# Query constants, transposition and last normalisation reordered, and the gated global row added to the residual by an accumulating transfer

## The reference

```
h   = layernorm(x) * (1 + ca) + sa
# attention inside segments of 128 tokens:
local      = softmax(Q K^T * scale) V              # per segment
global_out = attention over the 16 segments' first rows of the sequence
x   = x + ga * ((local + global_out[segment]) Wo + bo)
h   = layernorm(x) * (1 + cb) + sb
# 16 experts, each token goes to its best one, at most 512 tokens per expert
x   = x + gb * gate * (relu(h W1[e] + b1[e]) W2[e] + b2[e])
```

## Time and profile before

| | us |
|---|---|
| median of three runs | 1887.14 |
| the three runs | 1886.38 to 1889.94 |
| profiled execution | 1889.13 |
| span of its instructions | 1887.4 |

### The profile page before, as it was taken

One profiled execution on the slowest core, in us unless ns is written; L12 is line 12 of the kernel. 1 busy time (PEld: TensorE's weight loads), 2 busy tenths in 40 slices (PEclk: granted clock), 3 DMA queues, 4 the chain that ended last, 5 costly groups with the idle time before them and its releaser, 6 DMA issues.

```text
span 1887.4 us, 28151 instructions
## 1 busy us (share of the span) xinstructions
PE 1796.1 (95%) x9137; PEld 1486.9 (79%) x9138; DVE 1225.6 (65%) x1882; ACT 822.7 (44%) x1322; POOL 870.3 (46%) x709
## 2 busy tenths in 40 slices
PE   8999999999999549999999999999998999999998
PEld 3677787787787437888888888888888988888886
DVE  4568888888887753556554554537658886455762
ACT  2544554544554322433433343335545564334541
POOL 2145655656665441334343432416636757233632
PEclk9999999999999879999999999999999999999999
DMA  8322432342242524343535434345545455434622
GB/s 276 140 92 90 138 131 90 119 149 89 103 166 89 178 68 160 130 142 125 190 134 180 146 123 144 116 157 190 175 142 205 164 210 182 155 123 156 215 88 67
DMA packets 137915, 270.77 MB, mean 143 GB/s; under 512 B 17633, under 2 KB 18221, under 8 KB 137862
## 3 DMA queue, kind: packets, MB, share of 16 engines
q1 hardware_dynamic: 115338, 221.27, 33.6%
q0 software_dynamic: 22528, 48.86, 8.1%
HBM read 237.71 MB, written 50.72 MB: 153 GB/s over the span
## 4 chain that ended last, share of the span: by engine, by line
PE 77%; DVE 14%; issue 4%; ACT 3%; DMA 1%; POOL 0%; DVEq 0%; POOLq 0%; ACTq 0%; SPq 0%
PE bank L328 23%; PE bank L330 23%; PE bank L329 23%; PE bank L773 3%; DVE prob L1271 2%; DVE h L1377 2%; DVE xr L1381 2%; DVE stats L1156 2%; PE bank L715 1%; DVE u_lo L1399 1%; PE bank L816 1%; PE bank L598 1%; PE bank L536 1%; PE bank L587 1%; DVE h_lo L1438 0%
## 5 line engine op out<-in xcount | busy, mean ns | idle before, releaser
L1438 DVE TENSOR_TENSOR h_lo<-h_f,h_hi 128x512 fp32r<-128x512 f32 x256 | 221.3, 885 | 363.4 <-ACT h_f L1090 363.2
L1089 ACT ACTIVATE h_hi<-bank,b_col 128x512 fp32r<-128x512 f32 x256 | 176.4, 689 | 599.6 <-PE bank L330 582.1
L328 PE MATMUL bank<-bt_hi,w_hi 128*128 128x512 f32 (+4 forms) x1024 | 360.3, 352 | 8.4 <-DVE w_lo L1409 5.6
L330 PE MATMUL bank<-bt_hi,w_lo 128*128 128x512 f32 (+4 forms) x1024 | 359.4, 351 | 0.0
L329 PE MATMUL bank<-bt_lo,w_hi 128*128 128x512 f32 (+4 forms) x1024 | 359.4, 351 | 0.0
L328 PE MATMUL bank<-w_hi,h_hi 128*128 128x512 f32 x832 | 326.9, 393 | 3.3 <-DVE h_lo L1438 2.5
L329 PE MATMUL bank<-w_lo,h_hi 128*128 128x512 f32 x832 | 325.4, 391 | 0.0
L330 PE MATMUL bank<-w_hi,h_lo 128*128 128x512 f32 x832 | 324.9, 391 | 0.0
L328 PEld LDWEIGHTS bank<-bt_hi,w_hi 128*128 128x128 f32 x1024 | 194.7, 190 | 33.6 <-issue 9.6
L329 PEld LDWEIGHTS bank<-bt_lo,w_hi 128*128 128x128 f32 x1024 | 194.7, 190 | 21.0
L330 PEld LDWEIGHTS bank<-bt_hi,w_lo 128*128 128x128 f32 x1024 | 194.7, 190 | 20.3
(11 more groups left out here) (265 smaller groups left out, 3220.4 us busy)
## 6 DMA issues: line engine op xcount, KB each, us to landing
raw<-in_L_ffn_W_dram SPq DMA_DIRECT2D x128, 1024.0 KB, 5.5
xa<-in_L_attn_x_dram SPq DMA_DIRECT2D x16, 1024.0 KB, 5.3
xr<-in_L_attn_x_dram SPq DMA_DIRECT2D x16, 1024.0 KB, 8.1
out_dram<-xr SPq DMA_DIRECT2D x16, 1024.0 KB, 10.2
h_rows<-h SPq DMA_DIRECT2D x16, 1024.0 KB, 4.3
b_bc<-in_L_ffn_b_dram SPq DMA_DIRECT2D x16, 256.0 KB, 6.2
wm_a<-in_L_wmod_dram SPq DMA_DIRECT2D x2, 1024.0 KB, 11.1
wm_b<-in_L_wmod_dram SPq DMA_DIRECT2D x2, 1024.0 KB, 11.2
```

Source lines behind the costliest of these rows:

```text
L328: pe.matmul(o, a_hi, b_hi, start=start, stop=False)
L330: return pe.matmul(o, a_lo, b_hi, start=False, stop=stop)
L1089: act.activation(h1_hi[b % 2][:, j, :], h_bank[j][:, :], ACT.Relu, bias=bias)
L1438: dve.tensor_tensor(h1_lo[b % 2][:, j, :], h1_f[:, j, :], h1_hi[b % 2][:, j, :].bitcast(F32), ALU.subtract) \
```

## The change

Five things are edited.

1. The global row leaves PE. The prologue multiplies each global row by its `ga` row (a new product GAROW on PE, a copy on ACT, one multiplication on DVE in place of the four that split the row in three) and stores 64 float32 rows. In each iteration POOL issues a transfer that adds the four rows of group n-1 to the residual `xr`, each row to all 128 partitions; DVE waits for it (`xr_summed`) where it waited for the load of `xr`. The matmul L745, its two tiles and SP's load of `grows` go.
2. `query_const` is taken apart: three of its four rows stand right after `stats1`, the fourth after the second statistics, and the scaling after `u_lo` 0.
3. PE transposes the next `xa` before it multiplies the expert logits.
4. ACT does `modulate` before the fourth `normalise2`.
5. The scratch output of the query rows gets a tile of its own.

```diff
             if cur:
-                wait_past(sp, av_full, 4 * i.n - 4)
-                sp.dma_start(grows[i.par][0:3 * GS, :], global_dram[bass.ds(i.n * 3 * GS, 3 * GS), :]) \
-                    .then_inc(grows_in[i.par], 16)
...
-                    split3(pe, big[s][:, :], pt_hi[:, s, :], pt_lo[:, s, :], u_hi[:, s, :], u_lo[:, s, :], True, False)
-                    pe.matmul(big[s][:, :], seg_sel[:, s, :], grows[p1.par][:], start=False, stop=True) \
+                    split3(pe, big[s][:, :], pt_hi[:, s, :], pt_lo[:, s, :], u_hi[:, s, :], u_lo[:, s, :], True, True) \
                         .then_inc(av_full, 1)
...
+            if cur and not g_tiles:
+                pe.wait_ge(pro_evac, PRO_END)
+            if nxt:
+                transpose_xn(i.plus(1), False)
             if prev2:
                 pe.wait_ge(h2t_done, 4 * p2.n + 4)
...
-            if nxt:
-                transpose_xn(i.plus(1), False)
...
                 empty_u(3)
+            if nxt:
+                modulate(i.plus(1))
             if prev:
                 normalise2(3)
-            if nxt:
-                modulate(i.plus(1))
...
                 stats1(i.plus(1))
+            if cur:
+                for s in range(GS - 1):
+                    query_row(i, s)
...
-                dve.wait_ge(xr_in[p1.par], 16 * (p1.half + 1))
+                dve.wait_ge(xr_summed[p1.par], 16 * (p1.half + 1))
...
             if cur:
+                query_row(i, GS - 1)
                 for s in range(GS):
-                    if s == 2:
-                        query_const(i)
                     dve.wait_ge(u_hi_done, 4 * n + s + 1)
                     dve.tensor_tensor(u_lo[:, s, :], big[s][:, :], u_hi[:, s, :].bitcast(F32), ALU.subtract) \
                         .then_inc(u_split, 1)
+                    if s == 0:
+                        query_const(i)
...
+            def add_global():
+                pool.wait_ge(xr_in[p1.par], 16 * (p1.half + 1))
+                stand_alone(pool, pool_passed)
+                part = global_dram[bass.ds(p1.n * GS, GS), :].unsqueeze(0).to_broadcast([P, GS, D])
+                pool.dma_start(xr[p1.par][:], part, accum_op=ALU.add).then_inc(xr_summed[p1.par], 16)
+            first = isinstance(i.n, int) and i.n == 1
+            if prev and not first:
+                add_global()
             if nxt:
                 normalise1(i.plus(1))
+            if first:
+                pool.wait_ge(g_stored, 16)
+                add_global()
```

More of the change, by code:

```diff
@@ L123, in build_block @@
     ones = keep("ones", [P, P], BF16)
-    seg_sel = keep("seg_sel", [P, GS, P], BF16)
-    grows = [keep(f"grows{i}", [P, D], BF16) for i in range(2)]
+    seg_batch = keep("seg_batch", [NBATCH, NSEG], F32)
     QUAD = P // KC
@@ L179, in build_block @@
     prob, pt_hi, pt_lo = over(r_p, ("prob", seg_sq, F32), ("pt_hi", seg_sq, F32R), ("pt_lo", seg_sq, F32R))
-    logit_parts, = over(cursor[0], ("logit_parts", [P, ROWS], F32))
+    logit_parts, qc_junk = over(cursor[0], ("logit_parts", [P, ROWS], F32), ("qc_junk", [P, D], F32))
     batch_rows = [P, NBATCH, D]
@@ L199, in build_block @@
                                       ("bqk", [NBATCH, 2, D], F32), ("hg_t", [P, KC, NSEG], F32))
-    g_split, brow, u_row, gg_t = over(r_tab + 8 * KB, ("g_split", [NSEG, 3, D], BF16), ("brow", [P, D], F32),
+    g_ga, brow, u_row, gg_t = over(r_tab + 8 * KB, ("g_ga", [NSEG, D], F32), ("brow", [P, D], F32),
                                       ("u_row", [1, D], F32), ("gg_t", [P, KC, NSEG], F32))
@@ L263, in build_block @@
     gsum_masked, gsum_negb, gsum_exp, gsum_prob = (sem(f"gsum_{k}") for k in ("masked", "negb", "exp", "prob"))
-    g_split_done, g_stored, table_cleared = sem("g_split_done"), sem("g_stored"), sem("table_cleared")
+    g_gated, g_stored, table_cleared = (sem(k) for k in ("g_gated", "g_stored", "table_cleared"))
     x_in = [sem(f"x_in{i}") for i in range(2)]
     xr_in = [sem(f"xr_in{i}") for i in range(2)]
-    grows_in = [sem(f"grows_in{i}") for i in range(2)]
+    xr_summed = [sem(f"xr_summed{i}") for i in range(2)]
     ln1_step, ln1_ready, ln1_rstd, xn_done = (sem(k) for k in ("ln1_step", "ln1_ready", "ln1_rstd", "xn_done"))
@@ L346, in build_block @@
     POOL_MADE = 9
-    DVE_MADE = 9
+    DVE_MADE = 7
     def results_done(eng, e, b):
@@ L658, in _ @@
         product(PGT, pe.transpose(pro_bank(PGT)[:, 0:NSEG], pg[:], ident[0:NSEG, 0:NSEG]))
+        pe.wait_ge(mod_fixed, 2)
+        pe.wait_ge(made, POOL_MADE)
+        bank_free(GAROW)
+        product(GAROW, pe.matmul(pro_bank(GAROW)[0:NSEG, :], seg_batch[:], modr[:, GA, :], start=True, stop=True))
         pe.wait_ge(brow_ready, 1)
@@ L1263, in _, with query_row @@
         dve.wait_ge(made, POOL_MADE)
-        def query_const(g):
-            b = batch_of(g)
-            for s in range(GS):
-                if s > 0:
-                    dve.wait_ge(qc_raw, 4 * g.n + s)
-                dve.scalar_tensor_tensor(out=qc_junk, in0=xa[g.par][:, s, :], scalar=1.0,
-                                         in1=vc_tab[:, bass.ds(b, 1), :].rearrange("p b d -> p (b d)"), op0=ALU.mult,
-                                         op1=ALU.mult, accum_out=QRAW[:, s:s + 1]).then_inc(qc_raw, 1)
+        def query_row(g, s):
+            wait_past(dve, qc_raw, 4 * g.n + s)
+            dve.scalar_tensor_tensor(out=qc_junk[:], in0=xa[g.par][:, s, :], scalar=1.0,
+                                     in1=vc_tab[:, bass.ds(batch_of(g), 1), :].rearrange("p b d -> p (b d)"),
+                                     op0=ALU.mult, op1=ALU.mult, accum_out=QRAW[:, s:s + 1]).then_inc(qc_raw, 1)
+        def query_const(g):
             dve.wait_ge(qc_raw, 4 * g.n + 4)
-            dve.tensor_scalar(QCS2[g.par], QRAW, qc_bc[:, bass.ds(b, 1)], SCALE, ALU.add, ALU.mult) \
+            dve.tensor_scalar(QCS2[g.par], QRAW, qc_bc[:, bass.ds(batch_of(g), 1)], SCALE, ALU.add, ALU.mult) \
                 .then_inc(qc_ready, 1)
-        dve.wait_ge(g_split_done, 1)
         tok4 = [P, GS, E]
```

36 lines of the change are left out of this document (13 added, 23 removed).

## The result

The changed kernel takes 1896.38 us (median; 1893.87 to 1897.36), the kernel before 1889.65 beside it: 1.0033 of its time, 95% interval 1.0022 to 1.0044. That is slower by a third of a per cent, where 1880.4 was forecast; the sign was wrong.

A forecast was written before the change was run, and what follows sets the result against it. PE was taken to bound the attention part. -12.6 - 2.8 - 0.5 + 0 + 5.0 + 3.7 + 0.5 = -6.7 us, from the median 1887.14 to 1880.4 us; range 1869 to 1908.

The forecast's parts named there:

- Reordered end of an iteration, -12.6: Attention loop: transposing before the expert logits ends PE's wait for `u_lo`, 0.9 us gained in each of 14 iterations.
- The rival in which another input holds PE just as long: Loop: fourth `u_lo` or POOL's `h2` rows hold PE, only the transfer's costs stay; +6, 1893 us, chance 0.05.
- the prediction's own signs of being wrong: Loop: DVE's first `h` released by the transfer every iteration, or `pt_lo` no longer waiting for ACT; no size given.
- Matmul removed, -2.8: Loop, PE: 0.93 us of matmul saved per iteration, of which 0.2 was credited in each of iterations 2 to 15.
- The same transfer in iteration 1, +5.0: Iteration 1: the transfer, issued behind POOL's normalisation, delays `u` from 108.86 to 113.9; 5.0 us lost once.
- T: Accumulating transfer's time from issue to landing, taken as 6.0 us alone, between 4.7 and 7.3.
- The end, +3.7: Iteration 16: the transfer takes 10 us where DVE wants the sum after 6.3; 3.7 us lost.
- Steady transfer, 0: Steady iterations: the accumulating transfer is hidden before the next first `h`; 0 us.
- The 8.6: Steady iterations: the transfer's forecast time from issue to landing beside the store of `h2`, 8.6 us.
- The rival of a late transfer: Every iteration: the transfer lands after DVE wants it; about 1901 to 1916 us, chance 0.20.
- Query rows beside POOL's normalisation: Loop, DVE's gap: query rows collide with POOL's normalisation; as a rival all three collide, +7, 1894 us, chance 0.13.
- the prologue: Prologue and iteration 0: earlier transposition of group 1 less the added product and copy; 0.5 us gained.

The follow-up runs named there:

- the run with both transfers early: The changed kernel with the accumulating transfers of iteration 1 and of the last group (15) issued earlier; 1881.81 us, 0.9960 of the kernel before.
- the 1252.5 with the query rows put back: The kernel with first and last transfer early, its query rows put back between the second and third `u_lo`; 1910.63 us, 1.0117 of the kernel before.

## Why the prediction was wrong, step by step

- **Reordered end of an iteration, -12.6.** This step failed. The transposition's wait went as worked out, and `ht_lo` started 1.46 us earlier (14.60 after `h` against 16.06). But it ended only 0.49 earlier: its four instructions met more of POOL's scaling, which kept its place, and went from 1.27 to 1.74 us each. The end stayed because it hangs on POOL: 0.55 us behind the sixth scaling operation, which itself ended only 0.49 earlier (20.77 after `h` against 21.26). The prediction had POOL off the path with 1.65 us to spare; through `ht_lo` its scaling was on it. So 0.9 us an iteration became 0.2. The prediction asked what was due next on PE and named the fourth `u_lo`; what was due next was DVE's `ht_lo`, which the trace of before already shows stretched (213 to 570 us; the first row, beside its neighbour of equal size):

```profile
L1217 DVE TENSOR_TENSOR ht_lo<-ht,ht_hi 128x512 fp32r<-128x512 f32 x40 | 50.1, 1267 | 8.1 <-ACT ht L957 7.7
L1399 DVE TENSOR_TENSOR u_lo<-bank,u_hi 128x512 fp32r<-128x512 f32 x40 | 25.5, 678 | 0.0
```

  The rival in which another input holds PE just as long, given 0.05, had the right shape; it named the `h2` rows as PE's input, where POOL's scaling of them acts through `ht_lo`. One of the prediction's own signs of being wrong came true: `pt_lo` waits for ACT 0.5 us in 13 iterations, where it was 29.6.
- **Matmul removed, -2.8.** 0.06 to 0.12 us an iteration with the old orders (36.02 to 35.96 and 35.90), nothing on top of the new ones (35.79 to 35.81), where the period hangs on the end of `ht_lo` and DVE's chain from there to `h`.
- **The same transfer in iteration 1, +5.0.** Right in place, too small: moving it away saved 11.2. T was 8.3 and not 6.0, `h` can come 1.9 us earlier than in the kernel before (104.65 against 106.57), and the sum had no term for PE's clock after the stall, 1.9 on PE and at most 0.7 in the time.
- **The end, +3.7.** 3.3 by the run with both transfers early.
- **Steady transfer, 0.** Right. It lands 10.2 us after its issue at 423.61, near 433.8, and `h` starts at 435.73. The 8.6 was too low, the window just wide enough (12.1 from the issue). The rival of a late transfer is refuted. The Trainium skill (Collectives: The Full Stack, on the bandwidth ceiling) says of the reduce step of a ring collective, not of a kernel's own transfer, that its add needs two source reads and so runs at half the rate of a copy; 8.3 against 4.8 us, 1.73 times, comes near it.
- **Query rows beside POOL's normalisation.** Refuted as a cost: the rows take 0.69 in the new place, POOL's normalisation 0.78 a block as before, and only its inverse root grew, 1.03 to 1.44 us, off the path.
- **The sum.** The two waits cost 11.2 + 3.3 = 14.5. Without them the change is 7.1 faster (1881.81 against 1888.93), where -15.9 was forecast for the reorderings, the matmul and the prologue. So 8.8 us of the miss are gains that did not come, 5.3 are waits that were forecast at 9.2. That 1896.38 lies within the range of 1869 to 1908 is luck: the range reaches that far for late transfers and colliding query rows, and neither came. 14.5 - 7.1 = 7.4, against 6.7 measured directly (the kernel before moved by 0.7 between the two comparisons). Of the 7.1 the loop makes 14 x 0.19 = 2.7. Of the remaining 4.4 the profiles show 2.5 ahead of iteration 5 (249.03 - 245.69 = 3.3, less 0.8 of the loop's own): 1.2 at the first `h` of iteration 1, the rest in the four iterations from there; why these gain more than the loop was not taken apart. The last 1.9 is no more than the scatter: from the first `h` of iteration 16 to the end it is 1246.8 to 1250.1 us in the profiles of the table above, the 1252.5 with the query rows put back aside.

## What to carry to other kernels

Before crediting an instruction that starts earlier, look at what sets its end: a mean well above that of a neighbour of equal size is the sign of a shared resource, and moving the instruction deeper into that overlap gives the gain back. A two-operand VectorE subtraction that ran beside POOL was cheaper here with one operand in PSUM, even at the price of four more copies on a ScalarE that has time. A transfer that is hidden in the loop is priced again at the first and the last iteration, where its place in the queue and its company differ.

## What was not expected of the hardware

An accumulating 1 MB transfer lands in 8.3 us alone, 10.2 beside a 1 MB store and 11.0 beside a store and four loads; the plain copy takes 4.8 alone. In iteration 16 even tiny VectorE instructions stretched beside POOL's scaling, which ends at 635.99: two on four numbers per partition took 0.93 and 1.18 us, where the second takes 0.17 in the loop's iteration above (at 422.25). Both end 0.02 us behind one of POOL's operations (632.07 + 1.26 = 633.33, 633.29 + 1.26 = 634.55), as `ht_lo` does with 0.55: in these rows the VectorE instruction does not get through until POOL's has ended.

```profile
632.42 0.93 DVE L1338 SCALAR_TENSOR_TENSOR per_tok<-per_tok 128x4 f32<-128x4 f32 x1
633.38 1.18 DVE L1341 TENSOR_TENSOR per_tok<-per_tok 128x4 f32<-128x4 f32 x1
```

POOL beside them:

```profile
632.07 1.26 POOL L1624 TENSOR_TENSOR h<-h,sb_tab 128x512 f32<-128x512 f32 x1 [0.18 <-POOL h L1620]
633.29 1.26 POOL L1620 TENSOR_TENSOR h<-h,cb_tab 128x512 f32<-128x512 f32 x1
```
